# Weight preparation moved ahead of the second attention group, the post-attention stage of layer 0 pipelined over slices, its result passed on through DRAM

## What is computed

```python
x = _layernorm(x + _L0_attn_ref(x, ...))   # quaternion projections, 16 heads, full softmax over 4096 keys
x = _layernorm(x + _L0_ffn_ref(x, ...))    # rows of x and of the weight quantized to FP6 (blocks of 32), then xd @ wd.T + bias
x = _layernorm(x + _L1_attn_ref(x, ...))   # 16 query heads, 2 key heads, window of 256 keys
x = _layernorm(x + _L1_ffn_ref(x, ...))    # sigmoid(xr Wr) * (relu(xk Wk)^2 Wv), token shift in xr and xk
```

## Time and profile before

| | us |
|---|---|
| runs (2) | 5600.86 and 5631.44, median 5616.15 |
| the profiled execution | 5608.25 |
| its span on the slowest core (core 5) | 5606.7 |
| spans of the eight cores | 5581.3 to 5606.7 |
| mean granted TensorE clock, share of full | 0.651 to 0.659 |
| PE, DVE, ACT busy in the span | 2940.8, 1804.7, 1746.2 |

### The profile page before, as it was taken

One profiled execution on the slowest core, in us unless ns is written; L12 is line 12 of the kernel. 1 busy time (PEld: TensorE's weight loads), 2 busy tenths in 40 slices (PEclk: granted clock), 3 DMA queues, 4 the chain that ended last, 5 costly groups with the idle time before them and its releaser, 6 DMA issues.

```text
span 5606.7 us, 65780 instructions; the slowest of 8 cores (5581.3 to 5606.7 us)
## 1 busy us (share of the span) xinstructions
PE 2940.8 (52%) x18242; PEld 1424.5 (25%) x18242; DVE 1804.7 (32%) x4074; ACT 1746.2 (31%) x2188; POOL 158.6 (3%) x303
## 2 busy tenths in 40 slices
PE   0255257777775577777710333334466655555444
PEld 0122114444342243434310111111233322212112
DVE  0477310000001100000036555555355533334444
ACT  0000007777773277777710000000033210010000
POOL 0011010000000100000000000000000000000000
PEclk9976566666666666666655666666655556667656
DMA  1322230000001200000010000000100010001000
GB/s 15 75 34 31 45 45 1 4 4 4 4 4 26 38 4 4 2 3 4 4 53 22 17 17 17 17 17 6 23 12 7 12 31 12 12 18 30 25 21 23
DMA packets 130939, 104.58 MB, mean 19 GB/s; under 512 B 66568, under 2 KB 117424, under 8 KB 130608
## 3 DMA queue, kind: packets, MB, share of 16 engines
q0 software_dynamic: 42832, 45.15, 5.5%
q1 hardware_dynamic: 87776, 55.22, 3.5%
HBM read 112.91 MB, written 18.87 MB: 24 GB/s over the span
## 4 chain that ended last, share of the span: by engine, by line
PE 35%; ACT 24%; DVE 19%; issue 10%; DMA 8%; POOL 1%; DVEq 1%; ACTq 1%; SPq 0%; PEldq 0%; POOLq 0%
ACT TE L507 20%; PE PALL L531 8%; PE PALL L455 3%; PE PALL L325 2%; PE PALL L1081 2%; ACT TE L1057 2%; PE PALL L496 2%; PE PALL L739 2%; PE PALL L807 2%; PE PALL L1201 2%; DMA TY<-XFF 2%; PE PALL L1013 1%; PE PALL L1405 1%; DMA SMALL<-QBI 1%; PE PALL L1335 1%
## 5 line engine op out<-in xcount | busy, mean ns | idle before, releaser
L507 ACT ACTIVATE TE<-PALL,BIASB 128x768 bf16<-128x768 f32 x1536 | 1384.0, 901 | 842.1 <-PE PALL L496 705.8
L496 PE MATMUL PALL<-TY 64*128 64x384 bf16 x3072 | 864.9, 420 | 509.9 <-ACT TE L507 503.5
L496 PEld LDWEIGHTS PALL<-TY 64*128 64x128 bf16 x3072 | 299.8, 98 | 1042.2 <-issue 976.2
L531 PE MATMUL PALL<-TY,TE 128*128 128x65 bf16 x9216 | 447.3, 227 | 0.0
L531 PEld LDWEIGHTS PALL<-TY,TE 128*128 128x128 bf16 x9216 | 435.7, 121 | 32.1 <-issue 32.1
L325 PE MATMUL PALL<-TY,TE 128*128 128x512 bf16 (+1 forms) x832 | 219.2, 433 | 367.1 <-DVE TE L291 211.2
L543 DVE TENSOR_TENSOR PVAB<-PVAB,PALL 128x390 f32<-128x390 f32 x48 | 27.0, 562 | 878.8 <-PE PALL L531 860.1
L1057 ACT ACTIVATE TE<-PALL,BIASB 128x256 bf16<-128x256 f32 (+2 forms) x240 | 154.7, 645 | 425.8 <-PE PALL L1042 407.5
L455 PE MATMUL PALL<-TE,TY 128*128 128x512 bf16 x512 | 158.5, 466 | 243.3 <-DMA TY<-XFF 243.3
L538 DVE COPY PVAB<-PALL 128x390 f32<-128x390 f32 x48 | 27.1, 565 | 743.5 <-PE PALL L531 726.9
L785 PE MATMUL PALL<-IDB,TE 128*128 128x128 bf16 x144 | 38.2, 265 | 392.6 <-DVE TE L668 368.0
(11 more groups left out here) (179 smaller groups left out, 3398.0 us busy)
## 6 DMA issues: line engine op xcount, KB each, us to landing
TY<-XFF POOLq DMA_DIRECT2D x192, 128.0 KB, 4.6
TY<-XST SPq DMA_DIRECT2D x18, 512.0 KB, 3.5
YOUT<-TE SPq DMA_DIRECT2D x18, 512.0 KB, 2.6
ATT<-TY SPq DMA_DIRECT2D x36, 128.0 KB, 1.8
ATT<-TY SPq DMA_DIRECT2D x18, 256.0 KB, 2.3
TY<-QW SPq DMA_DIRECT2D x32, 128.0 KB, 2.5
TY<-KW SPq DMA_DIRECT2D x32, 128.0 KB, 2.5
TY<-XSF POOLq DMA_DIRECT2D x32, 128.0 KB, 5.6
```

The costliest lines, as they stand in the source:

```text
L496: t.matmul(o_, l_, r_, start=True, stop=True, tile_position=tp)),
L507: ss.activation(o_, i_, AF.Exp, bias=BIASB[:, 63:64], scale=0.125)),
L531: t.matmul(o_, l_, r_, start=s0, stop=False, skip_group_check=True)),
```

## The change

**Preparation** stands now between `emit_p1b(1)` and `emit_p1c(1)`. `quat_w3` has two staging slots for four, OW and the transposed FFN weight have other places in SBUF, and the identity matrices are loaded at the very start, ahead of the Q and K weights, which wait for that load. `emit_p1c` has a parameter `nsets`; the second group runs with two sets of score banks.

**Phase 2** is three functions: `p2_f1(sl)` (transposing loads, O projection, addition; now in banks 4 and 5), `p2_f2(sl)` (LN1, quantization), `p2_back(sl)` (transposes, FFN, LN2). They are called so that `p2_f1` runs two slices and `p2_f2` one slice ahead. LN2 writes bf16 rows, which a DMA on SP's queue stores to a DRAM tensor Y2SP; the eight fp32 transposes and copies into Y2 are gone. The x rows are loaded from POOL's queue into one buffer. The Square activations of LN1 and LN2 wait for the DVE sum.

**Layer 1** takes its input from Y2SP. Before each K and V block, and before each query tile, eight DMA transposes on SP's queue fill YSTG, in place of the eight DVE casts. **Phase 4** loads the slice's rows of Y2SP from POOL's queue, two buffers in turn, in place of the eight transposes and copies.

The core of the diff:

```diff
+        t_id = sch.dma("y", "dm", lambda y: y.dma_start(out=IDF, in_=IDENT),
+                       waits=[dm_chain[-1]])
+        dm_chain.append(t_id)
...
         quatw_lastv = [dm_chain[-1]] * 4
...
-        def emit_p1c(g, ready, state):
+        def emit_p1c(g, ready, state, nsets=3):
...
-                            par = sb % 3
+                            par = sb % nsets
...
+        def quat_w3(dst_fn, W_ap, firstw, stg_fn, extraw=()):
+            lastv = [firstw] * 2
...
+                    slot = ob % 2
...
+        wd_stage_free = None
+        wdt_done = None
         for oc in range(8):
-            wt = [t_id, two] + ([wd_stage_free] if wd_stage_free else [])
+            wt = [tg0] + g0_exps + ([wd_stage_free] if wd_stage_free else [])
...
+        st_p1c = emit_p1c(1, [v_done1], st_p1c, nsets=2)
...
+        def p2_f1(sl):
...
+                    w = [("dsp", sch.cnt["dsp"]), tg0]
+                    if p2s["oproj"].get(sl - 2):
+                        w.append(p2s["oproj"][sl - 2])
                 tldA = sch.dma("y", dl, (lambda y, s_=ATT0[128 * sl:128 * sl + 128,
                                                            128 * c:128 * c + 128],
                                          d_=AF0(p, c, 0, 128):
                                          y.dma_start_transpose(d_, s_)), waits=w)
...
+            t2ap = sch.op("v", (lambda v, z_=zap: v.tensor_scalar(XDF_AP, z_,
                                                           SMALL[:, 77:78], SMALL[:, 79:80],
                                                           ALU.add, ALU.mult)),
                           waits=[t2l2])
...
+            p2s["spill"][sl] = sch.dma("y", "dsp", (lambda y, r0=128 * sl:
+                                                    y.dma_start(out=Y2SP[r0:r0 + 128, :],
+                                                                in_=XDF_AP)),
+                                       waits=[t2ap])
+
+        p2_f1(0); p2_f2(0); p2_f1(1)
+        for sl in range(NSL):
+            p2_back(sl)
+            if sl + 1 < NSL:
+                p2_f2(sl + 1)
+            if sl + 2 < NSL:
+                p2_f1(sl + 2)
...
+                cast_tok = sch.dma("y", dls, (lambda y, d_=YSTG(ic, n),
+                                              s_=Y2SP[512 * si:512 * si + n,
+                                                      128 * ic:128 * ic + 128]:
+                                              y.dma_start_transpose(d_, s_)),
+                                   waits=w)
...
+                qcast = sch.dma("y", "dl0", (lambda y, d_=YSTG(ic, QT),
+                                             s_=Y2SP[qt * QT:(qt + 1) * QT,
+                                                     128 * ic:128 * ic + 128]:
+                                             y.dma_start_transpose(d_, s_)),
+                                waits=w)
...
+            ev_y2 = sch.dma("g", "dx0" if p == 0 else "dx1",
+                            (lambda g, d_=TEV(20480 + p * 2048, BF16, 1024),
+                             s_=Y2SP[128 * sl:128 * sl + 128, :]:
+                             g.dma_start(out=d_, in_=s_)), waits=w)
```

More of the change, by code:

```diff
@@ L693, in build_program, with QSLOT, Y1AP @@
             wdt_done = evs[-1]
[L694 removed]
+        st_p1c = emit_p1c(1, [v_done1], st_p1c, nsets=2)
+        att0_done = st_p1c["atm_free"]
+        tg1 = sch.op("t", lambda t: t.nop(), mark=True)
+        if stage == "p1c":
+            for sl in range(NSL):
+                sch.dma("g", "dout", (lambda gg, sl_=sl: gg.dma_start(
+                    out=DBG[:, sl_ * 1024: (sl_ + 1) * 1024],
+                    in_=ATT0[128 * sl_:128 * sl_ + 128, :])),
+                    waits=[("dsp", sch.cnt["dsp"])])
+            sch.op("y", lambda y: y.wait_ge(sem_handles["dout"], sch.cnt["dout"]))
+            sch.emit(block, sem_handles)
+            stack.close()
+            return nc
+        def QSLOT(i):
+            return TY2.bitcast(F32)[:, i * 1024:(i + 1) * 1024]
+        P2_SLOTS = (QSLOT(0), QSLOT(1), QSLOT(2), QSLOT(3))
+        XDT_AP = TY2.bitcast(BF16)[:, 8192:9216]
+        XDF_AP = TY2.bitcast(BF16)[:, 35072:36096]
+        def Y1AP(p):
+            off = 16384 if p == 0 else 24576
+            return TY3.bitcast(F32)[:, off // 4: off // 4 + 1024]
+        XTM_AP = TY3.bitcast(F32)[:, 20480 // 4: 20480 // 4 + 1024]
         def AF0(p, c, a, n):
[L697 removed]
+            base = (28672 + p * 2048) // 2
             return TY3.bitcast(BF16)[:, base + c * 128 + a: base + c * 128 + a + n]
[L700 to L708 removed]
+        p2s = {"oproj": {}, "y1evac": {}, "quant": {}, "transp": {},
+               "ffn0": {}, "z2": {}, "spill": {}, "ln2": {}}
+        def p2_f1(sl):
             p = sl % 2
             dl = "dl0" if p == 0 else "dl1"
[L711 removed]
             tldA = None
@@ L887, in build_program @@
                                         g.dma_start(out=d_, in_=s_)),
-                            waits=[tp2_nop, y2_done] if ic == 0 else [])
+                            waits=[tp2_nop] if ic == 0 else [])
         l_wk1 = None
@@ L1139, in build_program @@
                         waits=[tp3_nop])
-        if stage == "p4a":
-            for c in range(8):
-                sch.dma("g", "dout", (lambda gg, c_=c, q_=Y2C(c, 0, SPAN, F32): gg.dma_start(
-                    out=DBG[:, c_ * SPAN: (c_ + 1) * SPAN], in_=q_)),
-                    waits=[zc, l_b1o, ("da", sch.cnt["da"])])
-            sch.op("y", lambda y: y.wait_ge(sem_handles["dout"], sch.cnt["dout"]))
-            sch.emit(block, sem_handles)
-            stack.close()
-            return nc
         def AF1(p, c, a, n):
@@ L1155, in build_program @@
         af1_free = [None, None]
+        y2b_free = [None, None]
         y3_done = None
```

278 lines of the change are left out of this document (121 added, 157 removed).

## The result

| | before | after |
|---|---|---|
| median of the runs, us | 5590.77 (10 runs) | 5496.73 (11 runs) |
| lowest and highest | 5583.75, 5631.44 | 5487.41, 5521.61 |
| profiled execution, us | 5608.25 | 5492.11 |

The changed kernel is faster by 1.7%: ratio 0.983, 95% interval [0.9805, 0.9848], 94 us of the medians. The forecast was 5639 us, a small loss: 142 us too high and on the wrong side. The range of 5465 to 5720 holds the result, because it was drawn to reach rival A. 17 of the 142 us are no step's fault: the execution on which the sum was built lies 17 us above what is now the median of the kernel before. The other 125 lie in the steps.

A forecast was written before the change was run, and what follows sets the result against it. No engine has the span to itself; ACT limits attention, and phase 2 is a serial chain of DVE and PE. From 5608.25 us, 2 + 12 + 47 - 142 + 95 + 123 - 106 = +31 gives 5639 us, range 5465 to 5720.

The forecast's parts named there:

- rival A: Layer 1 loads: a transpose's issue doesn't depend on its size; sum -123, 5485 us, faster by 2.2%; chance 0.32.
- 1 start: Kernel start: the identity load stands ahead of the weight loads, which wait for it; +2 us.
- 0.44 + 0.76 per 128 rows: Layer 1 transposing loads: assumed SP issue time, 3.5 us at 512 rows, 2.7 and 2.0 for fewer.
- step 5: Layer 1 loads by DMA transpose, PE waits: K and V projections +95 us, Q projections +123.
- step 3: Second attention group: with two score sets, PV matmuls start one exp later per unit, cadence unchanged; +47 us.
- Step 4: Phase 2: slice period 38.5 us for 48.1, y2 transposes gone, O projection issued two slices ahead; -142 us.
- thin cover: Phase 2: spill, transposes and projection take 20.2 us against 20.4 of DVE work; 2 us later would cost 32.
- Step 2: Weight preparation: moved ahead of the second attention group, hides nothing; fewer OW slots +20, sum +12 us.
- step 6: Phase 4: transposes back go, so the O projection can start 6.2 us earlier in 17 slices; -106 us.
- Rival B: Layer 1 loads: issue proportional to size, 4.8 us at 512 rows; sum +119, 5727 us, slower by 2.1%; chance 0.11.
- C: Second attention group: the two-set score chain sets the pace, +67 us more, 5706 us; chance 0.07.
- D: Phase 2: the O projection just before keeps TensorE's clock up for FFN matmuls; -30, 5609 us; chance 0.06.

The follow-up runs named there:

- the run without the cover: Changed kernel with phase 2's slices in plain order, nothing of the next slice done by VectorE ahead of its loads and projection: 5850.81 us, ratio 1.046.

## Why the prediction was wrong

Step by step, forecast and measured:

| step | forecast | measured |
|---|---|---|
| 1 start | +2 | not visible: -11.5 on the two cores compared; the cores of one execution differ by 16 |
| 2 preparation | +12 | +8 |
| 3 two score sets | +47 | +76 |
| 4 phase 2 | -142 | -152 |
| 5 K and V | +95 | +28 |
| 5 Q | +123 | +52 |
| 6 phase 4 | -106 | -110 |
| sum of steps 2 to 6, and of all | +29, +31 | -98; -94 by the medians |

**The step that failed is 5, "I take 0.44 + 0.76 per 128 rows".** The split was right for one row count and wrong in its second half: 0.76 us is paid once per instruction. The issue is 1.26 us at 512 rows, not 3.5, and splitting the loads showed it directly (+133 for 104 more issues). By rival A's working this one term is 154 us too much (218 - 64); step 5 as a whole came out at 80 us for 218. It was named as the thing on which the 218 us hung, and rival A was the right one. That A's -123 us lie only 29 from the measured -94 is in part luck: it keeps step 3, which is 29 short, and the chain of step 5, 12 short, and phases 2 and 4 gave 14 more than forecast. I had built a value between two bounds by spreading a difference over rows, where the prediction itself noted that a plain DMA's issue is 0.44 us whatever it moves. That spoke for A, and was outweighed by nothing.

One size inside step 5 offset a part of that. With the three chained small loads it is 19.0 us from the last spill to the first transposing load, not 7.1; this is why K and V cost 28 where A's working gives 15. Moving them alone changed nothing, since the weights were next; the term was right that the chain stands ahead, and left out what stands beside it: the weights, and a spill that lands after 8 to 9 us.

**Step 3** had the mechanism right (one exp more at the end of each unit, the cadence kept) and the size off: it counted 47 and left out that PV would run slower. Restoring three sets gave back 77.6 us in the stage, doubling the edit cost another 76.

**Step 4** was right in its period (38.5 against 37.8 measured) and in the thin cover (0.2 us forecast; in the slice shown the projection ends 19.8 us after the normalization, the quantization 20.1), and the run without the cover showed 20.4 us a slice of exposure. The front of the stage is longer as forecast: the first normalization comes 60.5 us into it (60.8 by the prediction's terms), before 42.5.

**Step 2** was right that the preparation hides nothing where it stands (its 32 OW loads take 40.1 us, 42 forecast), and **step 6** that the transposes back stood on the path. Rival B fell with the split loads, C with the cadence, and D did not happen: the FFN matmuls of the slice above still take 3.57 us (3517.58) for the first eight and go fast only in the second.

```profile
3517.58 3.57 PE L830 MATMUL PALL<-TY 128*128 128x512 bf16 x8 [0.65 <-DVE TY L813]
```

Where did the gain of phases 2 and 4 (262 us) go? 76 into two score sets, 80 into PE's waits for layer 1's loads, 8 into preparation; 98 are left. The first came back with three sets, the second with a second buffer.

## What to carry to other kernels

- An instruction's cost measured at one size says nothing of how it scales. Before building a sum on it, look whether other instructions of its queue scale with size in the same trace. Here the plain ones did not, the transposing ones did not either, and 104 issues more for the same bytes cost 133 us.
- Moving a block of work ahead of another hides nothing as long as both stand in one order on every engine. Taken apart and placed in the gaps of engines that have room, the same work, 260 us as a block, lengthened the group by 1 us.
- A wait on a busy-looking page is a loss only where no other engine sets the pace (308.6 us in phase 2 for nothing, 94.5 us in layer 1 in full); and a load moved off the path saves only up to the next one that lands.

## What the runs showed of the hardware

- A transposing load holds the issuing queue for 1.23 us at 128 rows of 128 columns, 1.25 at 384 and 1.26 at 512, and lands 2.4 to 2.7 us after its issue (medians, changed kernel). Splitting 40 of them into 144 cost 133 us.
- An attention group with one bank set less has a granted clock of 0.58 for 0.63, in both places (changed kernel, and two sets in both groups), and its PV matmuls take 241 ns for 227. A structural wait of 1 us per unit so cost 1.6.
- Small loads chained behind each other's landing took 10.9, 4.3 and 2.9 us each beside GpSimd's weight loads, where the kernel before, without these beside them, issued them 3.4 and 2.0 us apart. A 256 KB store took 9.0 us to land there, for a median of 2.0 over the 18 slices (changed kernel).
